# First cross attention of a five-stage transformer kernel: the stacked keys go by way of DRAM instead of straight across SBUF

## What is computed

```
xn = layernorm(x, ln_x_g, ln_x_b)                    # x is the context here, 4 x 2048 x 512
ln = layernorm(latents, ln_l_g, ln_l_b)              # the 128 tokens of each batch
q = (ln @ Wq).reshape(b, m, h, d).transpose(0, 2, 1, 3)          # 16 heads of 64
kv = jnp.concatenate([xn @ Wkv, ln @ Wkv], axis=1)               # 2048 + 128 keys
qn = rmsnorm(q, qn_g) * scale
kn = rmsnorm(k, kn_g)
sim = jnp.einsum('bhid,bhjd->bhij', qn, kn)
attn = jax.nn.softmax(sim.astype(jnp.float32), axis=-1)
out = jnp.einsum('bhij,bhjd->bhid', attn, v)
```

## Time and profile before

| | before |
|---|---|
| median of 3 runs | 2803.84 us (2802.6 to 2809.68) |
| the profiled execution | 2801.7 us, its span 2799.9 us |
| TensorE busy | 2374.6 us, 85% |
| VectorE, ScalarE, GpSimd busy | 1852.6, 1597.2, 853.0 us |
| mean granted TensorE clock | 0.931 |

### The profile page before, as it was taken

One profiled execution on the slowest core, in us unless ns is written; L12 is line 12 of the kernel. 1 busy time (PEld: TensorE's weight loads), 2 busy tenths in 40 slices (PEclk: granted clock), 3 DMA queues, 4 the chain that ended last, 5 costly groups with the idle time before them and its releaser, 6 DMA issues. The chain is left out here.

```text
span 2799.9 us, 58295 instructions
## 1 busy us (share of the span) xinstructions
PE 2374.6 (85%) x21892; PEld 1539.0 (55%) x22210; DVE 1852.6 (66%) x4130; ACT 1597.2 (57%) x2934; POOL 853.0 (30%) x703
## 2 busy tenths in 40 slices
PE   4489999999999999997687789995589999996785
PEld 2235555555555556555335467773267676774442
DVE  4578777777777776664144289995577777663126
ACT  3246666666666666666223278983357777777113
POOL 2212333333433342234100000001456666656000
PEclk8699999999999999999887789998799999996887
DMA  3322233223322231111351179994443433221302
GB/s 123 104 59 67 70 108 87 66 68 111 87 65 67 78 86 42 38 35 30 128 183 63 36 288 371 361 361 137 152 131 114 127 118 126 84 86 35 121 1 77
DMA packets 256297, 314.16 MB, mean 112 GB/s; under 512 B 71424, under 2 KB 182912, under 8 KB 255120
## 3 DMA queue, kind: packets, MB, share of 16 engines
q1 hardware_dynamic: 252064, 302.28, 33.6%
q10 hardware_dynamic: 3312, 6.03, 0.6%
q0 software_dynamic: 640, 2.10, 0.3%
HBM read 226.56 MB, written 48.10 MB: 98 GB/s over the span
## 5 line engine op out<-in xcount | busy, mean ns | idle before, releaser
L571 POOL TENSOR_TENSOR a_plo<-a_p,a_phi 128x512 bf16<-128x512 f32 x272 | 323.3, 1189 | 766.0 <-ACT a_phi L627 764.7
L762 PE MATMUL ps<-w_lo,a_xhi 128*128 128x512 bf16 x1078 | 411.8, 382 | 2.0 <-issue 0.2
L761 PE MATMUL ps<-w_hi,a_xhi 128*128 128x512 bf16 x1054 | 402.9, 382 | 2.6
L763 PE MATMUL ps<-w_hi,a_xlo 128*128 128x512 bf16 x1039 | 396.7, 382 | 0.5
L1956 POOL TENSOR_TENSOR a_plo<-a_p,a_phi 128x512 bf16<-128x512 f32 x256 | 303.5, 1186 | 190.1 <-ACT a_phi L1993 185.7
L593 ACT ACTIVATE a_kraw<-ps 128x256 f32<-128x256 f32 x272 | 104.5, 384 | 402.9 <-PE ps L763 398.6
L650 DVE TENSOR_TENSOR a_v<-ps,a_v 128x256 bf16<-128x256 f32 x272 | 115.0, 423 | 237.5 <-ACT a_v L595 236.0
L2068 DVE CUSTOM_DVE_ANT_0 a_junk<-ps,a_biasrow 128x512 bf16<-128x512 f32 x256 | 176.3, 688 | 114.4 <-PE ps L2173 85.6
L1988 ACT ACTIVATE a_p<-ps,a_mcol 128x512 f32<-128x512 f32 x256 | 175.2, 684 | 100.9 <-PE ps L2191 94.7
L623 ACT ACTIVATE a_p<-ps,a_mcol 128x512 f32<-128x512 f32 x256 | 175.5, 686 | 20.6 <-PE ps L813 19.3
L695 DVE CUSTOM_DVE_ANT_0 a_junk<-ps,a_mrow 128x512 bf16<-128x512 f32 x256 | 174.7, 682 | 8.0 <-PE ps L793 4.8
(11 more groups left out here) (438 smaller groups left out, 6786.4 us busy)
## 6 DMA issues: line engine op xcount, KB each, us to landing
e_wst<-in_L_ffn_W SPq DMA_DIRECT2D x46, 2048.0 KB, 10.4
a_xn<-in_ctx SPq DMA_DIRECT2D x16, 1024.0 KB, 5.5
a_ks<-a_khi SPq DMA_DIRECT2D x256, 64.0 KB, 2.0
a_ks<-a_klo SPq DMA_DIRECT2D x256, 64.0 KB, 2.0
a_ct<-in_ctxT SPq DMA_DIRECT2D x16, 1024.0 KB, 5.5
a_ks<-k1h_d SPq DMA_DIRECT2D x128, 128.0 KB, 2.5
k1h_d<-a_khi SPq DMA_DIRECT2D x64, 128.0 KB, 2.0
k1l_d<-a_klo SPq DMA_DIRECT2D x64, 128.0 KB, 1.7
```

The costliest lines, as they stand in the source:

```text
L571: pool.tensor_tensor(p_lo[:, m % 3, :], p32[:, m % 2, :], p_hi[:, m % 3, :], ALU.subtract)\
L761: pe.matmul(out, x_hi[:, c, tile], w_hi[:, c, g, :], start=(c == 0), stop=False)
L762: pe.matmul(out, x_hi[:, c, tile], w_lo[:, c, g, :], start=False, stop=False)
L763: last = pe.matmul(out, x_lo[:, c, tile], w_hi[:, c, g, :], start=False, stop=(c == C - 1))
```

## The change

`stack` no longer copies the 64-row halves from `k_hi` and `k_lo` straight into `ks`. It first stores the whole 128-row block of the high part to a DRAM tensor of its own, then that of the low part, waits until both have landed, and reads the same four 64-row pieces back from DRAM onto the same rows of `ks`. The wait for the rows of two units before (`s_mm`) now stands behind the stores. The rest of the program is unchanged.

```diff
+    kd_out = [sem("a0_kd_out0"), sem("a0_kd_out1")]
...
             def stack(u, j, pr):
                 x = turn_index(u, j, pr)
+                w = 512 if j < 4 else 2 * P
+                sp.wait_ge(kthi_done, x + 1)
+                sp.dma_start(t["k0h_d"][x, :, 0:w], k_hi[:, x % KR, 0:w]).then_inc(kd_out[x % 2], 16)
+                sp.wait_ge(ktlo_done, x + 1)
+                sp.dma_start(t["k0l_d"][x, :, 0:w], k_lo[:, x % KR, 0:w]).then_inc(kd_out[x % 2], 16)
                 if u >= 2:
                     sp.wait_ge(s_mm, NT0 * (u - 2) + min(4 * j + 4, NT0))
-                for k, done, swap in ((k_hi, kthi_done, 0), (k_lo, ktlo_done, 1)):
-                    sp.wait_ge(done, x + 1)
+                sp.wait_ge(kd_out[x % 2], 32 * (x // 2 + 1))
+                for k, swap in ((t["k0h_d"], 0), (t["k0l_d"], 1)):
                     for half in range(2):
                         z = half ^ swap
-                        src = k[64 * half:64 * half + 64, x % KR, :]
+                        src = k[x, 64 * half:64 * half + 64, :]
...
+        t["k0h_d"] = nc.dram_tensor("k0h_d", (9 * UNITS, P, 512), BF16, kind="Internal").ap()
+        t["k0l_d"] = nc.dram_tensor("k0l_d", (9 * UNITS, P, 512), BF16, kind="Internal").ap()
```

## The result

| | before | after |
|---|---|---|
| median of 4 runs each, us | 2806.76 | 2885.43 |
| lowest and highest, us | 2802.6, 2810.91 | 2883.66, 2887.02 |
| span of the profiled execution, us | 2799.9 | 2882.9 |
| mean granted clock | 0.931 | 0.925 |

The change makes the kernel slower: ratio 1.0277, with 1.0259 to 1.0296 as its 95% interval, 79 us. I had forecast 2830 and a range of 2811 to 2862, so the direction was right and the size three times too small, outside the range.

The account below looks back on a forecast made before the run. TensorE's queue was taken to set the pace in the first cross attention. Late blocks, 9.3 (3,0) + 7.1 (0,1) + 9.8 (the rest) = 26 us on 2801.7, gave 2828; the median lies 2.1 higher: 2830, range 2811 to 2862.

Parts of the forecast that it names:

- the mechanism: First cross attention: copies wholly covered today; the longer path makes TensorE's first `maximum` wait for late blocks, 26 us in all.
- the quiet chain: Low part to landing without collisions: issue 0.03, store 1.7, three read issues 1.8, fourth read 2.3; 5.8 us, before about 2.6.
- (3,0): Key block (j,pr) with j = 3, pr = 0, used 5.64 us after its low part; lateness 9.3 us over all units.
- The cover of (0,1) by the value matmul's wait: TensorE's 1.42 us wait for `result` behind block j = 0, pr = 1 hides lateness; 7.1 us of its lateness left.
- term 2 of the chain: The store to its landing, seen as the next read's start: 1.7 us, from the second cross attention's blocks of the same size.
- Term 4: The fourth read of a block to its landing in `ks`: 2.3 us, bounds 2.0 and 2.5.
- What else is queued behind SyncE's new wait: Context stores, read-backs and context loads on SyncE: none comes within 4 us of its use, so they cost nothing.
- the clock, which is not in my sum: TensorE's granted clock, read as 1.00 (2.4 GHz) from 300 to 1040 us before the change; no cost was forecast for it.
- The slow one: Rival: stores and reads run at their means or slower, 48 to 69 us of loss, 2852 to 2873; chance 0.18.
- The cheap reads: Rival: read issues 0.43 apart, landings 2.2, chain 5.2; stalls nearly vanish, 8 to 11 us, 2812 to 2815; chance 0.2.
- A faster kernel by less interference with VectorE: Rival: without SBUF-to-SBUF copies VectorE's backlog shrinks and `turn`'s 26.6 us of stalls could go, 2777 at best; chance 0.02.
- Absorption in `turn`'s wait: Rival: TensorE's stalls are absorbed downstream in `turn`'s 26.6 us of waits, some 10 of 26 us remain, 2814; chance 0.05.

Follow-up runs that it names:

- runs 4 and 5: Against the changed kernel: 4 has every `maximum` one step later, 2825.6 us; 5 has the six query loads one step later, behind the stack's work, 2861.95 us.
- Run 9: The changed kernel with one read per block, query and context loads later and every `maximum` one step later: 2802.52 us, ratio 0.9982 to the kernel before.
- run 2: The changed kernel with its four reads per block taken from SBUF again, behind the same stores and wait: 2883.83 us, ratio 1.0289 to the kernel before.

## Why the prediction was wrong

**Right: the mechanism, and the quiet chain.** Nobody waited for the copies before, and the new wait is on DMAs from `k0l_d`. The chain of a quiet block was 0.03 + 1.7 + 1.8 + 2.3 = 5.8 by the prediction, and 0.03 + 1.74 + 1.8 + 2.4 = 6.0 in the rows. In (3,0), units 4 to 8 came late by 0.10 to 0.19 where I had 0.2. That all of (3,0) came to 9.9 us where I had 9.3 is luck: units 0 and 1 have 4.4 (I had 2.3), units 9 to 14 4.5 (I had 0.8), and units 2, 3 and 15, where I had 5.0, have 0.35. The cover of (0,1) by the value matmul's wait was real: 14.2 us went away with the change, and 10 to 13 came back in runs 4 and 5, where (0,1) was less late. SyncE's waits behind the stores are, in the stage (us in total, times, longest):

```profile
SPq L472 <- DMA k0l_d<-a_klo: 241.7, 126, 7.0
...
SPq L478 <- DMA k0l_d<-a_klo: 25.9, 16, 3.6
```

I had 1.4 for each, some 200 in all; 268 over 142 is 1.9. The Trainium skill ("DMA: Bandwidth & Descriptors", anatomy of one DMA) would have a store of 128 KB at 2.3 as an estimate; its fit there is of DMAs issued by GpSimd, and these are issued by SyncE. In the traces a store with nothing beside it takes some 1.8 and the mean of all 144 is 2.37. The loss of 49 by that estimate would have been nearer than mine, but for another reason than the one that the runs show.

**Wrong, first: term 2 of the chain, "I take 1.7".** The 1.7 was minimum and median of another stage's stores. Here 30 of 144 stores took 3.0 us or more, 17 with a fetch of instructions in flight and 13 behind a large transfer. Their tail was in the row that I quoted, a mean of 2.03 and a longest of 4.1, and I priced it as a rival with the same excess for all, not as a tail that meets some blocks. It makes a block late by itself: (0,0) has 9.2 us where I had 3.9, and (0,1) of unit 11 has 4.15 where I had 0.9, with its own store at 4.07. It also reaches the next block by way of the queue: in unit 8 the store of (0,0) took 3.61, and (0,1), behind it, was late by 5.61 where I had 2.9. In units 4 and 12 (0,1) was late by 4.97 and 4.83 where I had 2.5 and 2.3; there single issues on SyncE took longer (2.26 for a pair of reads, 1.20 for a store), and the rest isn't assigned. Term 4 had the same fault on a smaller scale: 2.9 to 3.3 instead of 2.3 in five blocks (3,0).

**Wrong, second: "What else is queued behind SyncE's new wait ... they cost nothing."** I had asked only whether the context loads and read-backs come late for their own use. They don't: no wait of a matmul for them is in the view. But delayed behind (0,1)'s reads they go out just ahead of (1,0)'s store, which in unit 7 landed 7.6 us later. In units 2, 3, 5, 7 and 10 a context load stands so, and these are 10.2 of (1,0)'s 10.9 us, where I had none.

Lateness in all is 75.5 against 39 (19.8 + 9.3 + 9.8). With the cover taken off it is 56 against 26, so these two steps, with the small terms beside them, are 30 us of the miss.

**Wrong, third, and the largest single term: the clock, which is not in my sum.** I took the earlier trace rows with its clock of 1.00 as fixed. There are 61.5 us more at half clock, TensorE is busy for 50.5 of them, and that costs some 25. Run 9, with gaps of 1.1 us, has 6.8 us at half clock. Run 4, with gaps of 14.3 in all, has 27.3, but 10.2 of these follow `turn`'s gap of some 5 us that the kernel before has too.

**Rivals.** The slow one, 2852 to 2873, was nearest, but not by the measured path: quiet blocks ran nearly as forecast, and collisions and clock made the difference. The cheap reads fell with the first row of two issues (1.09 and 1.24 for a pair, 0.6 each). A faster kernel by less interference with VectorE: `turn`'s wait did shrink by 4.3, but run 2, with copies from SBUF, has 22.2 as well, so it isn't the source of the reads. That the gaps elsewhere give VectorE time to catch up would explain it, but no run shows it. Absorption in `turn`'s wait: 4.3 of 26.6.

Still open is whether the instruction fetches cause the 3.5 us of the 24 stores, and where the 7 us went that the account leaves.

## What to carry to other kernels

A wait put into a queue that other transfers share is paid by the block with the least cover, and by the store that stands behind the transfers it delays: lay out the queue again with the delay in it, and ask what each large transfer now stands ahead of. Price a landing by its spread under this stage's traffic, not by its minimum, and add to the longer gaps of TensorE the half-clock stretches behind them (here some 25 us beside 74.5). And where a late block is covered by another wait behind it, take that wait away first: it was worth 20 us here, and the change nothing.

## What the runs showed of the hardware that I had not expected

- From a store of 128 KB from SBUF to DRAM to the first read behind its landing it was 1.84 us in the median where neither of the following was there (102 of 144), 3.52 with an instruction fetch of 16 KB in flight (24), and 4.60, up to 7.6, within 7 us behind loads of 0.5 to 1 MB (18).
- Reads of 64 rows onto the stack cost the same from DRAM as from SBUF (79 us and 80 us of loss behind the same wait; 73 to 83 and 71 to 91 by their intervals).
- Gaps of 2.0 to 5.6 us in an otherwise full queue of TensorE went with 3.4 to 6.8 us at 1.2 GHz each, though some of 2.0 to 2.5 us had none. As an estimate they cost some 23 us beside 74.5 us of gaps.
- One read of 128 partitions and 256 rows in all was issued in 0.40 us, where four of 64 took 0.5 to 0.6 each.
